# Cross-attention: three of four blocks weighed in two parts, each behind half of another block's scores, and turned maxima a chunk later

## What is computed

```python
x = x + xattn(layernorm(x), ctx)      # x (16, 64, 512), ctx (16, 1601, 512)
def xattn(x, y):                      # 16 heads of 32
    q, k, v = split_heads(x @ Wq), split_heads(y @ Wk), split_heads(y @ Wv)
    attn = softmax(einsum('bhid,bhjd->bhij', q, k) * SCALE, axis=-1)
    return merge_heads(einsum('bhij,bhjd->bhid', attn, v)) @ Wp + bp
```

## Time and profile before

| | us |
|---|---|
| median of 3 runs (lowest, highest) | 1891.07 (1890.6, 1891.12) |
| the profiled execution: its own time | 1889.2 |
| the profiled execution: span from the first to the last instruction | 1887.1 |
| busy in the span: TensorE / VectorE / GpSimd / ScalarE | 1840.6 / 1116.1 / 884.9 / 833.3 |
| mean granted TensorE clock | 0.996 of full |

### The profile page before, as it was taken

How to read it: one execution, slowest core, us unless ns; L and a number is a source line. 1 busy time by engine, 2 the same in 40 slices (tenths; PEclk the granted TensorE clock), 3 DMA queues, 4 the chain that set the end, 5 groups by cost and what they waited for, 6 DMA issues and landing times. The chain is left out here.

```text
span 1887.1 us, 65530 instructions
## 1 busy us (share of the span) xinstructions
PE 1840.6 (98%) x28992; PEld 1585.5 (84%) x28992; DVE 1116.1 (59%) x1353; ACT 833.3 (44%) x1031; POOL 884.9 (47%) x830
## 2 busy tenths in 40 slices
PE   6999999999999999999999999999999989999998
PEld 3979898989898989898888888888888867777887
DVE  4475656566565656574747484848483757473265
ACT  4444444444444545454545353535353524343322
POOL 0192727363636454545555454636363754344111
PEclk9999999999999999999999999999999999999999
DMA  5200202020202010110102020202020231122110
GB/s 214 86 4 3 78 3 77 3 77 3 77 6 74 13 68 29 51 46 34 60 21 74 6 78 3 78 2 78 2 78 2 69 129 46 24 91 89 45 56 23
DMA packets 40202, 94.53 MB, mean 50 GB/s; under 512 B 18688, under 2 KB 20224, under 8 KB 39936
## 3 DMA queue, kind: packets, MB, share of 16 engines
q1 hardware_dynamic: 39936, 90.26, 13.5%
HBM read 81.99 MB, written 6.16 MB: 47 GB/s over the span
## 5 line engine op out<-in xcount | busy, mean ns | idle before, releaser
L416 POOL TENSOR_TENSOR fold<-fold,prob 128x256 f32<-128x256 f32 (+1 forms) x704 | 705.9, 1003 | 55.2
L98 PE MATMUL ring<-y_parts,w_keep 128*128 128x402 f32 (+1 forms) x3072 | 607.4, 351 | 1.4 <-PEq L173 1.4
L98 PE MATMUL ring<-wv_s,y_parts 128*128 128x512 f32 (+1 forms) x2496 | 596.2, 396 | 0.0
L98 PEld LDWEIGHTS ring<-y_parts,w_keep 128*128 128x128 f32 x3072 | 551.3, 188 | 17.1 <-issue 3.5
L98 PEld LDWEIGHTS ring<-wv_s,y_parts 128*128 128x128 f32 (+1 forms) x2496 | 453.8, 184 | 112.6
L410 POOL TENSOR_TENSOR fold<-prob 128x256 f32<-128x256 f32 x64 | 68.4, 1069 | 697.4 <-ACT prob L453 697.4
L430 ACT ACTIVATE k_sb<-ring 128x402 f32<-128x402 f32 (+1 forms) x256 | 129.4, 505 | 372.4 <-PE ring L98 372.4
L570 DVE TENSOR_TENSOR prob<-prob,peak_rows 128x1024 f32<-128x1024 f32 (+1 forms) x192 | 278.0, 1500 | 12.1 <-ACT peak_rows L449 12.1
L443 ACT ACTIVATE prob<-s_ps 128x1536 f32<-128x1536 f32 (+1 forms) x128 | 199.9, 1561 | 128.0 <-PE s_ps L693 128.0
L453 ACT ACTIVATE prob<-prob 128x1024 f32<-128x1024 f32 (+1 forms) x192 | 207.5, 1123 | 3.2 <-DVE prob L570 1.2
L547 DVE TENSOR_TENSOR fold<-prob 128x512 f32<-128x512 f32 x64 | 51.9, 811 | 228.2 <-ACT prob L443 228.2
(11 more groups left out here) (191 smaller groups left out, 1487.1 us busy)
## 6 DMA issues: line engine op xcount, KB each, us to landing
y_raw<-yT SPq DMA_DIRECT2D x48, 804.0 KB, 6.2
y_raw<-yT SPq DMA_DIRECT2D x16, 792.0 KB, 9.9
f_raw<-w_ffn SPq DMA_DIRECT2D x22, 512.0 KB, 3.3
p_x<-x SPq DMA_DIRECT2D x2, 1024.0 KB, 7.4
q_scratch<-p_x SPq DMA_DIRECT2D x4, 512.0 KB, 2.7
q_sb<-q_scratch SPq DMA_DIRECT2D x16, 128.0 KB, 8.5
x_sb<-x SPq DMA_DIRECT2D x4, 512.0 KB, 7.5
aw_raw<-y_raw SPq DMA_DIRECT2D x8, 256.0 KB, 3.7
```

Of the source, the lines that this page charges most:

```text
L98: mm = pe.matmul(out, left(a, c), right(b, c), start=(c == 0 and n == 0), stop=(c == DC - 1 and n == 2))
L416: pool.tensor_tensor(acc[0:m], acc[0:m], prob[0:m, i, t, :], ALU.add).then_inc(sum_step, 1)
```

## The change

The weighing of blocks 1, 2 and 3 of the batch before is cut in two at a row tile: block 1 at tile 8, blocks 2 and 3 at tile 6. Each part stands directly behind one half of another block's scores, with no chunk of keys or values between them. Block 0 stays whole where it was. The `turn` of blocks 0, 1 and 2 moves behind one more chunk, with its `spread_peaks` a chunk behind it as before; `turn` and scores, which stood together, are now apart. In the values stage everything from `turn(b, 2)` on stands one value tile later. ScalarE's and VectorE's lists follow: `exponential`, `peak_row`, `peaks`, `subtract` and `output` move by one or a few places, and VectorE copies value tile 4 before the second part of block 3's tree, not behind it.

The diff, cut to TensorE's list, VectorE's from the middle of the keys stage on, and the place in ScalarE's values stage that stands ahead of block 2's exponentials:

ScalarE, values stage:

```diff
             def values_phase(b, more):
                 score(b, 3, 0)
+                exponential(b, 1, 2)
                 value(b, 1)
                 peak_row(b, 2)
                 score(b, 3, 1)
+                value(b, 3)
                 exponential(b, 2, 0)
                 exponential(b, 2, 1)
                 exponential(b, 2, 2)
-                value(b, 3)
                 if more:
                     high(b + 1, 0)
```

VectorE, values stage:

```diff
-            def values_phase(b, more):
+                largest(b, 1, 0)
+                peaks(b, 0)
+                subtract(b, 0)
+                largest(b, 1, 1)
+                if past:
+                    output(b - 1, 2)
+                largest(b, 2, 0)
+                peaks(b, 1)
+                subtract(b, 1)
+                largest(b, 2, 1)
+
+            def values_phase(b, past, more):
                 value(b, 0)
+                if past:
+                    output(b - 1, 3)
+                largest(b, 3, 0)
                 peaks(b, 2)
-                largest(b, 3, 0)
+                value(b, 2)
                 subtract(b, 2)
-                value(b, 2)
+                value(b, 4)
                 largest(b, 3, 1)
-                value(b, 4)
                 if more:
                     low(b + 1, 0)
+                value(b, 6)
                 peaks(b, 3)
-                value(b, 6)
-                subtract(b, 3)
-                value(b, 8)
                 if more:
                     low(b + 1, 1)
                 else:
                     dve.wait_ge(wp_hi, 1)
                     dve.tensor_tensor(y.keep[:, 1], y.w_raw, y.keep[:, 0].bitcast(F32), ALU.subtract)
+                value(b, 8)
+                subtract(b, 3)
                 value(b, 10)
```

TensorE:

```diff
-            def weigh(b, i, at=small_ps):
+            def weigh(b, i, first=0, end=JT, at=small_ps):
                 block = NBLK * b + i
                 if i == 0:
                     pe.wait_ge(act_out, ACT_N * (b + 1))
                     pe.wait_ge(dve_out, DVE_N * (b + 1))
-                pe.wait_ge(exp_ok, len(PIECES) * (block + 1))
-                for t in range(JT):
+                if first == 0:
+                    pe.wait_ge(exp_ok, len(PIECES) * (block + 1))
+                for t in range(first, end):
                     m = jtile(t)
                     for g in range(HB):
                         pe.matmul(at[g * DH:(g + 1) * DH, 0:N], v_sb[0:m, t, (HB * i + g) * DH:(HB * i + g + 1) * DH],
                                   prob[0:m, i, t, g * N:(g + 1) * N], start=(t == 0), stop=(t == JT - 1))
+                if end < JT:
+                    return
                 pe.wait_ge(sum_step, SUMS * (block + 1))
                 for g in range(HB):
                     mm = pe.matmul(at[g * DH:(g + 1) * DH, N:2 * N], ones[:, 0:DH], fold[:, i, g * N:(g + 1) * N],
@@ -732,6 +753,8 @@
                 mm.then_inc(pv_ok, 1)
             def batch(b, past):
                 keys(b, 0, 0)
                 keys(b, 0, 1)
                 if past:
@@ -741,46 +764,61 @@
                 keys(b, 0, 3)
                 keys(b, 1, 0)
                 scores(b, 0, 0)
+                if past:
+                    small_output(b - 1, 0)
+                    weigh(b - 1, 1, 0, 8)
                 keys(b, 1, 1)
                 scores(b, 0, 1)
+                if past:
+                    weigh(b - 1, 1, 8)
                 keys(b, 1, 2)
+                keys(b, 1, 3)
+                keys(b, 2, 0)
+                scores(b, 1, 0)
+                keys(b, 2, 1)
                 if past:
-                    small_output(b - 1, 0)
-                    weigh(b - 1, 1)
-                keys(b, 1, 3)
-                for i in (2, 3):
-                    keys(b, i, 0)
-                    if past:
-                        small_output(b - 1, i - 1)
-                    else:
-                        small_rows(b, i - 3)
-                    turn(b, i - 2)
-                    scores(b, i - 1, 0)
-                    keys(b, i, 1)
-                    spread_peaks(b, i - 2)
-                    scores(b, i - 1, 1)
-                    keys(b, i, 2)
-                    if past:
-                        small_rows(b, i - 2)
-                        weigh(b - 1, i)
-                    keys(b, i, 3)
+                    small_output(b - 1, 1)
+                turn(b, 0)
+                keys(b, 2, 2)
+                spread_peaks(b, 0)
+                scores(b, 1, 1)
+                small_rows(b, 0)
+                if past:
+                    weigh(b - 1, 2, 0, 6)
+                keys(b, 2, 3)
+                keys(b, 3, 0)
+                scores(b, 2, 0)
+                if past:
+                    weigh(b - 1, 2, 6)
+                keys(b, 3, 1)
+                if past:
+                    small_output(b - 1, 2)
+                turn(b, 1)
+                keys(b, 3, 2)
+                spread_peaks(b, 1)
+                scores(b, 2, 1)
+                small_rows(b, 1)
+                if past:
+                    weigh(b - 1, 3, 0, 6)
+                keys(b, 3, 3)
                 values(b, 0)
                 scores(b, 3, 0)
                 if past:
+                    weigh(b - 1, 3, 6)
+                values(b, 1)
+                if past:
                     small_output(b - 1, 3)
-                else:
-                    small_rows(b, 1)
                 turn(b, 2)
-                values(b, 1)
+                values(b, 2)
                 spread_peaks(b, 2)
                 scores(b, 3, 1)
-                for t in range(2, 6):
+                for t in range(3, 7):
                     values(b, t)
                 small_rows(b, 2)
                 turn(b, 3)
-                values(b, 6)
+                values(b, 7)
                 spread_peaks(b, 3)
-                for t in range(7, JT):
+                for t in range(8, JT):
                     values(b, t)
```

More of the change, by code:

```diff
@@ L467, in keys_phase @@
                     key(b, 0, c)
-                for i in range(1, NBLK):
-                    key(b, i, 0)
-                    score(b, i - 1, 0)
-                    key(b, i, 1)
-                    if i >= 2:
-                        peak_row(b, i - 2)
-                    score(b, i - 1, 1)
-                    key(b, i, 2)
-                    if i >= 2:
-                        exponential(b, i - 2, 0)
-                        exponential(b, i - 2, 1)
-                    key(b, i, 3)
-                    if i >= 2:
-                        exponential(b, i - 2, 2)
+                key(b, 1, 0)
+                score(b, 0, 0)
+                key(b, 1, 1)
+                score(b, 0, 1)
+                key(b, 1, 2)
+                key(b, 1, 3)
+                key(b, 2, 0)
+                score(b, 1, 0)
+                key(b, 2, 1)
+                key(b, 2, 2)
+                peak_row(b, 0)
+                score(b, 1, 1)
+                exponential(b, 0, 0)
+                key(b, 2, 3)
+                exponential(b, 0, 1)
+                key(b, 3, 0)
+                score(b, 2, 0)
+                exponential(b, 0, 2)
+                key(b, 3, 1)
+                key(b, 3, 2)
+                peak_row(b, 1)
+                score(b, 2, 1)
+                exponential(b, 1, 0)
+                key(b, 3, 3)
+                exponential(b, 1, 1)
             def values_phase(b, more):
                 score(b, 3, 0)
+                exponential(b, 1, 2)
                 value(b, 1)
@@ L497, in values_phase @@
                 value(b, 5)
-                peak_row(b, 3)
                 if more:
@@ L503, in values_phase @@
                 value(b, 7)
+                peak_row(b, 3)
+                value(b, 9)
                 exponential(b, 3, 0)
@@ L506, in values_phase @@
                 exponential(b, 3, 2)
-                value(b, 9)
                 if more:
@@ L597, in keys_phase @@
                 largest(b, 0, 1)
-                for i in (1, 2):
-                    peaks(b, i - 1)
-                    largest(b, i, 0)
-                    subtract(b, i - 1)
-                    largest(b, i, 1)
-                    if past:
-                        output(b - 1, i + 1)
-            def values_phase(b, more):
+                largest(b, 1, 0)
[9 more added lines that the diff above has]
+            def values_phase(b, past, more):
                 value(b, 0)
+                if past:
+                    output(b - 1, 3)
+                largest(b, 3, 0)
                 peaks(b, 2)
-                largest(b, 3, 0)
+                value(b, 2)
                 subtract(b, 2)
-                value(b, 2)
+                value(b, 4)
                 largest(b, 3, 1)
-                value(b, 4)
                 if more:
                     low(b + 1, 0)
+                value(b, 6)
                 peaks(b, 3)
-                value(b, 6)
-                subtract(b, 3)
-                value(b, 8)
                 if more:
@@ L636, in _ @@
```

(8 more changed lines are left out.)

1 line of the change is left out of this document (removed).

## The result

| kernel | median us (lowest, highest) | to the kernel before [95% interval] |
|---|---|---|
| before | 1890.84 (1889.41, 1891.12) | |
| after | 1946.65 (1944.73, 1949.31) | 1.0296 [1.0281, 1.0312] |

The account below looks back on a forecast made before the run. TensorE, busy all 92.61 us of a batch, was taken as the bound. Per batch -0.15 + 0.63 + 0.20 = +0.68, times 15 = +10.2, less 1.2 in the first batch: +9.0, a median of 1900.1 us (own range 1896 to 1904).

Parts of the forecast that it names:

- TensorE's own list: TensorE's matmuls per batch: splitting weighings (W) behind halves of scores (S) and parting turns from scores gives -0.15 us.
- T of block 3: Values stage: block 3's `turn` waits for VectorE's tree, slowed by a GpSimd add; 0.63 us late per batch.
- P of block 3: Block 3's `spread_peaks` waits for VectorE's `low`, copy of tile 6 and `peaks`; about 0.2 us late per batch.
- First batch: The batch that weighs nothing: TensorE's 1.82 us wait for block 2's tree shrinks, 1.2 us off (bounds 0.6 and 1.8).
- S to W dearer: Rival: changing from scores to weighing on TensorE costs more, +0.54 us per batch, 1908 us; 8%.
- the add misses the tree: Rival: VectorE's first fold beats GpSimd's add, block 3's turn 0.13 us late, -0.02 per batch, 1889.6 us; 17%.

Follow-up runs that it names:

- the wide pair: Kernel before and changed kernel, each with every tile of scores as one matmul of 128 weights, not two of 64: 1931.29 and 1937.18 us.
- short: tree_first with the weighing of blocks 1 to 3 cut so that no run between chunks holds over 272 instructions (was 320): 1897.09 us.
- tree_first: Changed kernel with VectorE's copy of value tile 4 behind block 3's tree again: 1933.16 us.
- the moved kernels: Changed kernel with small matmuls ahead of the first batch, 208, 352, 112 or 176 instructions: 1941.34, 1923.80, 1920.71, 2032.21 us.

## Why the prediction was wrong

The sum was made of four terms. Three were near, the fourth was 3 us too high over the run, and a fifth was missing.

*TensorE's own list, -0.15 per batch: right.* A part of W starts 1.18 behind an S. One batch has 92.50 us of busy time against 92.61. Cleaner, from the wide pair: 1433.33 - 1427.03 = 6.3, less 15 turns' waits of 0.59, leaves -2.5, which is 15 x -0.17. And short came out at my sum.

*T of block 3 late by 0.63: right in kind and nearly in size, 0.60.* TensorE's timeline around it, VectorE's behind the copy of tile 4, and GpSimd's (its last two rows are single adds, from narrow windows):

```profile
204.71 11.39 PE L98 MATMUL ring<-wv_s,y_parts 128*128 128x512 f32 x48
...
216.67 3.04 PE L98 MATMUL ring<-wv_s,y_parts 128*128 128x512 f32 x12
```

```profile
210.58 0.69 DVE L548 COPY v_sb<-ring 128x512 f32<-128x512 f32 x1 [2.63 <-PE ring L98]
211.18 3.47 DVE L566 TENSOR_TENSOR fold<-fold,prob 128x512 f32<-128x512 f32 x3
214.69 0.85 DVE L568 TENSOR_TENSOR fold<-fold 128x256 f32<-128x256 f32 x1
215.57 0.85 DVE L570 TENSOR_TENSOR fold<-fold,prob 65x256 f32<-65x256 f32 x1
216.34 1.82 DVE L600 TENSOR_TENSOR y_parts<-y_raw,y_parts 128x1608 fp32r<-128x1608 f32 x1
```

```profile
209.42 0.75 POOL L410 TENSOR_TENSOR fold<-prob 128x256 f32<-128x256 f32 x1 [5.10 <-ACT prob L453]
210.25 12.00 POOL L416 TENSOR_TENSOR fold<-fold,prob 128x256 f32<-128x256 f32 x9
...
211.07 0.74 POOL L416 TENSOR_TENSOR fold<-fold,prob 128x256 f32<-128x256 f32 x1
...
216.21 2.55 POOL L416 TENSOR_TENSOR fold<-fold,prob 128x256 f32<-128x256 f32 x1
```

T's unhindered start is read between starts: 210.01 - 198.78 = 11.23 behind the first of the four tiles, here at 204.71 + 11.23 = 215.94. The tree starts 4.76 ahead of that, to the hundredth what I had. GpSimd's third add starts at 211.07, 0.11 ahead of the tree, where I had 0.15, and the tree lasts 216.42 - 211.18 = 5.24, which is my 4.74 + 0.50: the three folds take 3.47 where they took 2.96. T follows its end after 0.05, not 0.15, so it is 216.47 - 215.94 = 0.53 late and not 0.63; and the tile behind it starts 0.20 behind T (216.67), where in tree_first, without the wait, it is 0.13. Together 0.60. The 0.38 on TensorE's row is less because the modelled end of the matmul ahead of T hides the rest.

*P of block 3 late by 0.2: wrong.* `low` at 216.34 took 1.82, unslowed, and P didn't wait. The step that failed: "starts right behind a slowed fold, where GpSimd's next add is due". The add was due, its row even starts 0.13 ahead of `low`'s, but here it was the add that was held up, 2.55 us, and not `low`.

*First batch, -1.2: -0.9.* The turn of block 2 there waits 0.16 in place of the 1.82 of the earlier trace rows, and starts at 103.09. The turn of block 3 waits in this batch too, 0.28 by the page, which I had not counted.

*What was missing.* The step that failed is the first: "two things alone can change the time: how long its own list takes, and a wait that it has not now", with the list costed by what the array does. A third resource feeds it: the stream of instructions. In the kernel before the longest runs without a chunk hold some 230 instructions (a W has 224), so that each block of 256 has some of a chunk's 24 in it. A block with 24 of a chunk's instructions takes at least 2.19 + 116 x 0.0142 = 3.8 us, more than the 3.61 in which one arrives. The change made six runs of 320 per batch, and 256 of these take 1.8.

The missing term is 49.8 us in the 15 batches, 3.3 per batch: this is read between starts, each stretch of the loop against the same stretch of the moved kernels where no stop falls in it. 23.9 of it are at the first stop, 10.7 at the second, 11.4 at the third and the rest at small stops elsewhere. The page shows 33.6 of it as idle, since modelled ends hide the beginning of each stop. So the loop's +56.6 is 49.8 for the stops, 15 x 0.60 = 9.0 for the turn's wait, and -2.2 for the list.

The rivals were all about which engine is late or what the array does, and none held this. It could have been priced from the trace of before: its stops end at 1530.66 and 1534.41, 3.75 us apart with 128 matmuls between them, and that is the price. "S to W dearer" reached 1908 and was the nearest, by a mechanism that isn't there. One slip in the rivals changes nothing: where the add misses the tree, 15 x -0.02 belongs to the sum, which gives 1889.3 and not 1889.6.

## What to carry to other kernels

Count instructions as well as array time: where small matmuls stand together, ask how long the engine takes for 256 instructions in a row (matmuls and weight loads), and if that is under about 3.6 us, expect stops, marked "issue" within a group of equal instructions and always at the same places of a loop, each ending a little over 1 us behind the landing of a 16 KiB instruction packet. Large matmuls between small ones pay for the refill, so here spreading small groups was worth more than joining them: a change in and out of small tiles costs 0.22 us, a stop in the changed kernel's loop up to 1.8. Before a version with such runs is called better or worse by a few per cent, move its loop by some instructions: here that alone moved the time by 5.8%.

## What the hardware showed that I had not expected

- A block of 256 instructions every 3.61 us in a dense run, with a stop of 1.47 to 1.76 each time. The packet for the next block starts about 1 us after a block is entered, so the engine holds the block in work and one more; I infer this from the packets' times, no run sets it by itself. With several blocks held no stop would be expected in the loop, since that batch takes 95.7 us for 3347 instructions, 7.3 per 256. On this the Trainium skill has two figures ("Runtime: NRT & Kernel Launch", Instruction fetch mechanics): 2048 instructions held for TensorE, and two blocks of 256. The stops agree with the second.
- While the next context is loaded a refill starts late: 7.8 to 9.9 us after the block is entered, against 1.1 in the median away from a load, and 2.73 us of waiting with the DMA engines at 0.82, against 1.6 at most in the changed kernel's loop. The packet itself takes no longer. What holds it back is not shown. The stop was followed by a granted clock of 0.65 over 4.8 us, so it cost more than its length.
- A matmul of 128 weights with 32 rows is no cheaper way to write two of 64: the loop of before took 39 us longer with them, though it issued half the matmuls in S (x18422 against x24662 in the loop as a whole).
